# Compact inversion of the weight sums in the last attention, and layer norms that carry additions, clearing, loads and binarizing

## The reference

```python
x = x + jnp.tanh(g_xattn[3]) * _L3_xattn_ref(_layernorm(x, axis=-1), ctx_768, ...)
x = x + jnp.tanh(g_ffn[3]) * _L3_ffn_ref(_layernorm(x, axis=-1), ...)
```

```python
attn = jnp.einsum('bhqd,bhkd->bhqk', q, k) * scale
attn = jnp.clip(attn, -CLAMP, CLAMP)
attn = jax.nn.softmax(attn, axis=-1)
attn = jnp.where(jnp.any(jnp.isnan(attn)), jnp.asarray(1.0 / Nkv, attn.dtype), attn)
x = jnp.einsum('bhqk,bhkd->bqhd', attn, v).reshape(B, Nq, Cq)
return x @ Wo + bo
```

```python
alpha = mean(abs(w), axis=1, keepdims=True); bw = alpha * sign(w)      # _binarize
h = jax.nn.gelu(jnp.einsum('bsd,hd->bsh', x, bw1) + b1, approximate=False)
out = jnp.einsum('bsh,dh->bsd', h, bw2) + b2
```

## Time and profile before

| | |
|---|---|
| median of 3 runs | 4717.48 us (4715.63 to 4719.13) |
| the profiled execution | 4710.85 us, of it span 4709.2 us |
| last attention's loop, first clip to last | 3637 to 4591 us of the span |
| last norm and network | 4639 to 4705 us |
| mean granted TensorE clock | 0.892 of 2.4 GHz |

### The profile page before, as it was taken

One profiled execution on the slowest core, in us unless ns is written; L12 is line 12 of the kernel. 1 busy time (PEld: TensorE's weight loads), 2 busy tenths in 40 slices (PEclk: granted clock), 3 DMA queues, 4 the chain that ended last, 5 costly groups with the idle time before them and its releaser, 6 DMA issues. The chain is left out here.

```text
span 4709.2 us, 86688 instructions
## 1 busy us (share of the span) xinstructions
PE 3802.0 (81%) x32862; PEld 2475.0 (53%) x32862; DVE 2832.7 (60%) x3540; ACT 2051.6 (44%) x2875; POOL 1444.2 (31%) x1905
## 2 busy tenths in 40 slices
PE   7389889952557999997999996499585888888875
PEld 7156556631334666664666663277332555555553
DVE  8566555643335555534555543477546999989982
ACT  7166666630112434332343442266222666656651
POOL 0265344303213223212332310022005555545510
PEclk9689999976867999997999997799796999989996
DMA  6166666633413323312332320111004665556620
GB/s 165 44 149 151 136 140 146 149 104 134 149 24 90 87 79 85 80 47 62 87 87 79 86 61 15 41 44 31 17 0 100 138 137 129 133 124 138 138 71 14
DMA packets 197062, 434.60 MB, mean 92 GB/s; under 512 B 45708, under 2 KB 98878, under 8 KB 196589
## 3 DMA queue, kind: packets, MB, share of 16 engines
q1 hardware_dynamic: 122196, 338.87, 28.7%
q0 software_dynamic: 38912, 47.06, 4.7%
q10 hardware_dynamic: 35616, 43.97, 3.5%
HBM read 244.72 MB, written 32.67 MB: 59 GB/s over the span
## 5 line engine op out<-in xcount | busy, mean ns | idle before, releaser
L1401 DVE TENSOR_REDUCE L_mp<-ps 112x2 f32<-112x1000 f32 x384 | 458.2, 1198 | 549.4 <-PE ps L1223 545.9
L1260 PE MATMUL ps<-L_p,L_cn 125*97 125x448 f32 x1536 | 639.2, 538 | 0.0
L1384 ACT ACTIVATE L_p<-ps 125x896 f32<-125x896 f32 x384 | 352.2, 917 | 634.5 <-PE ps L1248 562.1
L2064 DVE TENSOR_REDUCE L_mp<-ps 112x2 f32<-112x1000 f32 x384 | 456.4, 1193 | 72.1 <-PE ps L1865 57.0
L2030 ACT ACTIVATE L_p<-L_p 125x896 f32<-125x896 f32 x384 | 364.8, 950 | 258.1 <-DVE L_p L2081 257.1
L885 ACT ACTIVATE L_p<-ps,rk 125x896 f32<-125x896 f32 x384 | 385.8, 1005 | 164.3 <-PE ps L763 144.9
L2081 DVE SCALAR_TENSOR_TENSOR L_p<-ps,xn 125x896 f32<-125x896 f32 x384 | 414.9, 1081 | 28.9 <-DMA xn<-L_low 20.2
L1246 PE MATMUL ps<-L_qh,L_ch 97*125 97x448 f32 x768 | 385.7, 502 | 14.2 <-DMA L_qh<-L_mc 14.2
L1260 PEld LDWEIGHTS ps<-L_p,L_cn 125*97 125x97 f32 x1536 | 250.4, 163 | 205.8 <-issue 165.9
L1897 PE MATMUL ps<-L_p,L_vs 125*18 125x112 f32 x6144 | 233.5, 272 | 120.2 <-ACT L_p L2030 104.5
L1223 PE MATMUL ps<-L_cr,L_qb 96*112 96x500 f32 x768 | 271.6, 440 | 37.8 <-DMA L_cr<-in_ctxT 32.6
(11 more groups left out here) (518 smaller groups left out, 7185.8 us busy)
## 6 DMA issues: line engine op xcount, KB each, us to landing
L_ks<-L_k_part SPq DMA_DIRECT2D x288, 375.0 KB, 9.7
L_ks<-L_k_first SPq DMA_DIRECT2D x96, 375.0 KB, 7.1
moe_w<-in_L_w SPq DMA_DIRECT2D x64, 512.0 KB
L_cn<-in_ctxN SPq DMA_DIRECT2D x32, 568.4 KB
cs_ct<-in_ctxT SPq DMA_DIRECT2D x32, 562.5 KB
L_raw<-in_ctxT SPq DMA_DIRECT2D x32, 562.5 KB
L_cr<-in_ctxT POOLq DMA_DIRECT2D x32, 562.5 KB, 4.8
L_ch<-in_ctxT POOLq DMA_DIRECT2D x32, 562.5 KB
```

The source lines that it names most:

```text
L1260: mm = nc.tensor.matmul(U[:, a, :], CN[s][:, j, :], P[:, n % 2, a * HALF:(a + 1) * HALF], start=(j == 0), stop=(j == KT - 1))
L1384: nc.scalar.activation(two(P[:, n % 2, :]), SB[n % 2], ACT.Exp).then_inc(S["exped"].sem, 1)
L1401: nc.vector.tensor_reduce(mp[:, 2 * k:2 * k + 2], ps[0:TT, bank:bank + 2, 0:500], AX.X, ALU.max).then_inc(S["chunk_maxed"].sem, 1)
L2064: nc.vector.tensor_reduce(mp[:, 2 * c:2 * c + 2], ps[0:TT, CB[pair], 0:500], AX.X, ALU.max).then_inc(S["chunk_maxed"], 1)
```

## The change

- `new_signals(True)` opens no block: the old semaphores are kept in `core.done`, and the next layer norm has GpSimd clear them beside its work.
- `add_gated` is gone. In the layer norms ahead of the four networks, VectorE adds one group of 448 columns at a time (`add`), and TensorE waits for each group before it makes its mean. The order on VectorE is add 0, add 1, centring 0, add 2, centring 1, add 3, centring 2, centring 3.
- `fold_weights` (second attention) and `quantize_weights` (third) give their loads to the layer norm ahead of them; in the former SyncE also waits there for their landing.
- `binarized_mlp` runs its layer norm itself and gives it the loads, the sign (ahead of the squares on ScalarE), the binarizing (between centring and inversion on VectorE), the transposes (behind the spreads on TensorE, now in banks 5 and 6) and the copy (at the end on VectorE).
- In the last attention the sums are picked out by four small matmuls with `UE` as weights into 112 partitions x 16 columns. VectorE inverts those 16 columns once, behind the clip of step 3. ScalarE widens them to 2 x 256 columns (`widen`, ahead of the key part and the exp of step 5; they are stored in `RD` and `UN`), TensorE transposes and spreads them with four matmuls at step 5 (`spread`), and ScalarE copies the 448 columns to `RD` ahead of the exp of step 7 (`take_sums`).

```diff
-        if old:
+        if later:
+            self.done += old
+        elif old:
...
+            if done:
+                @block.gpsimd
+                def _(pool):
+                    nc.clear_and_free_semaphores([s.sem for s in done])
...
                 for c in range(NCH):
+                    if gated:
+                        pe.wait_ge(added.sem, added.at(c + 1))
                     nc.tensor.matmul(ps[:, c, 0:CH], core.J[:, :], src[:, columns(c)],
...
+                if aside:
+                    aside.tensor(pe)
...
+                if aside:
+                    aside.scalar(act)
                 for c in range(NCH):
                     act.wait_ge(cen.sem, cen.at(c + 1))
...
+                if gated:
+                    add(0)
                 for c in range(NCH):
+                    if gated and c + 1 < NCH:
+                        add(c + 1)
                     dve.wait_ge(mean.sem, mean.at(c + 1))
...
+                if aside:
+                    aside.vector(dve, link)
                 dve.wait_ge(cen.sem, cen.at(NCH))
                 dve.wait_ge(std.sem, std.at(1))
...
-    MISC = {0: ("keys", 0), 1: ("keys", 1), 2: ("keys", 2), 3: ("pair", 0), 6: ("turn", 0),
+    MISC = {0: ("keys", 0), 1: ("keys", 1), 2: ("keys", 2), 3: ("pair", 0), 5: ("spread", 0), 6: ("turn", 0),
...
+            def pick_sums(b):
+                pe.wait_ge(S["u_copied"], b.lin(1, 2))
+                for c in range(4):
+                    mm = nc.tensor.matmul(ps[0:2 * NQ, 5, 4 * c:4 * c + 4], UE[:, c // 2, c % 2 * 2 * NQ:][:, 0:2 * NQ],
+                                          core.ident[:, DH:128:32], start=True, stop=True)
+                mm.then_inc(S["sums_picked"], 1)
 
             def spread_sums(b):
-                pe.wait_ge(S["u_copied"], b.lin(1, 2))
-                for j in range(2):
-                    mm = nc.tensor.matmul(of_head(ps[:, 5, 0:2 * QV], j), core.sum_row[:, j, :],
-                                          of_head(UE[:, :, :].rearrange("p s n -> p (s n)"), j),
-                                          start=True, stop=True)
+                pe.wait_ge(S["sums_widened"], twice_half_of(b, 2))
+                for c in range(4):
+                    mm = nc.tensor.matmul(ps[:, 5, c * 2 * NQ:(c + 1) * 2 * NQ],
+                                          wide(c // 2)[:, c % 2 * 128:(c % 2 + 1) * 128],
+                                          core.ident[0:2 * NQ, 0:2 * NQ], start=True, stop=True)
                 mm.then_inc(S["sums_spread"], 1)
...
+            def widen(b):
+                act.wait_ge(S["sums_inverted"], half_of(b, 1))
+                if b.turn is not None or b.r:
+                    act.wait_ge(S["u_normed"], b.lin(1, 0))
+                    act.wait_ge(S["projected"], half_of(b, 0))
+                for n in range(2):
+                    nc.scalar.activation(wide(n).rearrange("p (c g d) -> p c g d", c=2, g=4),
+                                         RC[:, 2 * n:2 * n + 2, :].unsqueeze(3).to_broadcast([2 * NQ, 2, 4, 32]),
+                                         ACT.Copy).then_inc(S["sums_widened"], 1)
...
+                    if n == 5 and b.r % 2 == 0 and (b - 2).there():
+                        widen(b - 2)
                     for at, c in ((5, 0), (7, 1), (8, 2)):
                         if n == at and (b + 3).there():
                             second_of_keys(b + 3, c)
...
-                nc.vector.reciprocal(RD[:, s, :], ps[:, 5, s * QV:(s + 1) * QV]).then_inc(S["sums_inverted"], 1)
+                nc.vector.reciprocal(RC[:, :, :].rearrange("p c g -> p (c g)"), ps[0:2 * NQ, 5, 0:16]
+                                     ).then_inc(S["sums_inverted"], 1)
...
-        layer_norm(core, core.OT, core.xn, "o0", gamma_beta)
-        add_gated(core, core.xn, 0)
-        core.new_signals()
-        layer_norm(core, core.xT, core.xn, "f0")
+        layer_norm(core, core.OT, core.xn, "o0", gamma_beta)
+        core.new_signals(True)
+        layer_norm(core, core.xT, core.xn, "f0", gated=(core.xn, 0))
```

More of the change, by code:

```diff
@@ L70, in __init__ @@
         self.eps = self.sb("eps", [128, 1])
-        self.signals, self.part = [], 0
+        self.signals, self.done, self.part = [], [], 0
         self.new_signals()
@@ L217, in _, with add @@
                 link = core.linker(dve, "dve")
+                def add(c):
+                    tile, gate = gated
+                    nc.vector.scalar_tensor_tensor(out=core.xT[:, columns(c)], in0=tile[:, columns(c)],
+                                                   scalar=core.tg[:, gate:gate + 1], in1=core.xT[:, columns(c)],
+                                                   op0=ALU.mult, op1=ALU.add).then_inc(added.sem, 1)
+                if gated:
+                    add(0)
                 for c in range(NCH):
+                    if gated and c + 1 < NCH:
+                        add(c + 1)
                     dve.wait_ge(mean.sem, mean.at(c + 1))
@@ L229, in _ @@
                     finish(link)
-        for s, n in ((mean, NCH), (cen, NCH), (sq, NCH), (var, 1), (std, 1), (inv, 1), (spread, NCH)):
+                if aside:
+                    aside.vector_last(dve, link)
+        for s, n in ((added, NCH if gated else 0), (mean, NCH), (cen, NCH), (sq, NCH), (var, 1), (std, 1), (inv, 1), (spread, NCH)):
             s.base += n
[L234 to L243, removed]
 CS = 4
@@ L416, in fold_weights, with load @@
         nw = 16 * len(loads)
-        with nc.Block() as block:
[L418 to L422, removed]
+        def load(sp):
+            for dst, name in loads:
+                sp.dma_start(dst, d[f"{L}_{name}"]).then_inc(w_in.sem, 16)
+            sp.wait_ge(w_in.sem, nw)
+        if norm:
+            norm(load)
+        with nc.Block() as block:
+            if not norm:
+                block.sync(load)
             if N is None and not keep_max:
@@ L1610, in misc @@
         kind, n = MISC[k]
+        if kind == "spread" and b.r % 2:
+            return None
         if kind == "pair":
             kind = "project" if b.r % 2 else "sums"
-        of = {"values": b + 1, "keys": b + 3, "turn": b + 1, "sums": b - 2, "project": b - 3}[kind]
+        of = {"values": b + 1, "keys": b + 3, "turn": b + 1, "sums": b - 2, "spread": b - 2, "project": b - 3}[kind]
         if not of.there():
@@ L1849, in fifth_bank @@
                 if kind == "sums":
+                    pick_sums(of)
+                if kind == "spread":
                     spread_sums(of)
@@ L1954, in _ @@
             pe.wait_ge(*emptied("project", 0, last - 2))
+            pick_sums(last)
             spread_sums(last)
@@ L2014, in empty @@
                     copy_turned(of)
+                if kind == "spread":
+                    take_sums(of)
                 if kind == "project":
@@ L2049, in _ @@
             copy_sums(Eight(None, B - 1))
+            widen(Eight(None, B - 2))
+            take_sums(Eight(None, B - 2))
             out(Eight(None, B - 2))
@@ L2104, in body @@
                         clip_tile(b + 1, k + 2 - KT)
-                    if b.r % 2 == 0 and (b - 2).there() and k in (3, 4):
-                        invert(b - 2, k - 3)
+                    if b.r % 2 == 0 and (b - 2).there() and k == 3:
+                        invert(b - 2)
             first = Eight(None, 0)
@@ L2122, in _ @@
             batches(dve, body)
-            for s in range(2):
-                invert(Eight(None, B - 2), s)
+            invert(Eight(None, B - 2))
             dve.wait_ge(S["u_normed"], B)
@@ L2607, in loads @@
             sp.dma_start(wd[:, :, :], d[f"{L}_wd"]).then_inc(S["wd_in"], 16)
-        layer_norm(core, core.xT, core.xn, tag, loads=loads)
+        layer_norm(core, core.xT, core.xn, tag, loads=loads, gated=gated)
         with nc.Block() as block:
@@ L2878, in quantize_weights, with load @@
         w_in, summed, spread = (core.sig(f"bitw_{n}") for n in ("in", "summed", "spread"))
+        def load(sp):
+            for n in BW:
+                sp.dma_start(w[n][:, :, :], d[f"bit_{n}"]).then_inc(w_in.sem, 16)
+        if norm:
+            norm(load)
         with nc.Block() as block:
-            @block.sync
-            def _(sp):
-                for n in BW:
-                    sp.dma_start(w[n][:, :, :], d[f"bit_{n}"]).then_inc(w_in.sem, 16)
+            if not norm:
+                block.sync(load)
             @block.tensor
```

110 lines of the change are left out of this document (61 added, 49 removed).

## The result

The changed kernel takes 4658.8 us (median of four, 4651.6 to 4677.9) against 4716.6 of the kernel before (four runs): a ratio of 0.9885, 95% interval 0.9855 to 0.9916, so 54 us less, between 40 and 68. A second comparison of the same two gave 4664.9 against 4711.1, ratio 0.9905 (0.9887 to 0.9922), 45 us less, between 37 and 53. Forecast were 4670 and 48 us.

What follows compares the result with a forecast made beforehand. No engine was full over the span; VectorE bound odd batches, even ones were slowed by TensorE's clock, and nothing overlapped at seams. Seams 34 plus loop 14 made 48 us off the 4717.48 median: 4670, range 4645 to 4698.

Steps and rivals of the forecast that it cites:

- seam term: Where blocks end and layer norms begin: additions, clearing, loads and last stage together save 34 us, bounds 27 to 43.
- loop term: Last attention's loop: 1.1 us saved per pair of batches, 15 in all, minus 1.5 at the tail: 14 us.
- Additions: Four seams with an addition ahead of a norm: quarter additions overlapping the norm save 2.0 us each, 8 in all.
- Clearing: Four other seams: semaphore clearing beside the norm saves 0 to 0.94 us each, taken as 2 in all.
- Loads: Weight loads covered by the preceding norm: 11.1 us saved at the second attention, 5.7 at the third.
- Last stage: Final norm to first matmul: 13.45 us now, new sum 6.4 including a 2.95 later inversion, so 7.1 saved.
- The failed term: Even batches of the last attention: TensorE falling to 1.2 GHz costs 1.3 us, counted for half, so 0.6 per pair.
- Limits and keys: Last attention's loop: transfers of limit vector and keys lose the slow stretch as slack, costing 0.3 us per pair.
- Tail: End of the last attention, at 1.2 GHz: a longer chain of pick, invert, widen, spread and copy loses 1.5 us.
- The second (the loop gives nothing, the clock falls each time): Rival for the last attention's loop: exponential 5 late, clock falling each time, only seams count; 4683.5 us, chance 0.22.
- The first (clock holds everywhere): Rival for the last attention's loop: the clock holds, the loop gives 26.5 us, time 4657; chance 0.24.
- The third: Rival: the new gap keeps TensorE at 1.2 GHz from tile 5 to 10; slower, 4766 us, chance 0.05.

Runs made afterwards that it cites:

- the second execution: The changed kernel profiled again, unaltered, with the second comparison against the kernel before: span 4654.4 us, median 4664.9 us, ratio 0.9905.
- the first execution: The changed kernel's first profiled execution, the longest of its four: 4677.9 us, span 4676.3 us.
- the seams alone: The whole change, but with the last attention's loop as in the kernel before: 4671.9 us, ratio 0.9918 to the kernel before.
- gap-filled kernel: The changed kernel plus five matmuls of 500 columns, results unread, in TensorE's idle piece of even batches: 4639.2 us, ratio 0.9853.
- the kernel with the earlier turn: The changed kernel with ScalarE's widening moved behind tile 5's exponential and the limits' turn at place 4 instead of 6: 4601.2 us, ratio 0.9767.
- the loop alone: The last attention as changed, all seams as in the kernel before: 4707.7 us, ratio 0.9991 to the kernel before.
- the long gap: The changed kernel with widening behind tile 5's exponential, plus fourteen small ScalarE copies ahead of that exponential in even batches: 4690.9 us, ratio 0.9948.
- the widening later: The changed kernel with ScalarE's widening one place later, behind tile 5's exponential: 4616.9 us, ratio 0.9798 to the kernel before.
- the old gap: The changed kernel with widening behind tile 5's exponential, plus seven small ScalarE copies that make that exponential late again: 4667.4 us, ratio 0.9915.

## Why the prediction came out, point by point

The total was right in part by luck: a seam term that was too small and a loop term that was too large nearly cancelled. In both, the term mis-sized most is TensorE's clock.

**Additions.** Forecast 8 us, 2.0 each. The four blocks take 5.87, 7.09, 5.88 and 6.98 us in the profile (9.43, 9.98, 9.82 and 9.26 before): 12.7 saved. I had put the last centring's end at 7.1 to 8.0. The step that failed is the first mean, "its centring 1.87 us later": that row was taken at a granted clock of 0.50, and I used it for all four blocks. In the second and the fourth block the clock is 0.50 there again; the first centring starts 2.64 us behind the first addition (forecast 2.6), and quarter 3's addition ends at 5.35 and 5.25 (forecast about 5.4). In the first and the third the clock is 1.00: the first mean takes 1.05 us, the first centring starts at 1.79, and quarter 3's addition ends at 4.14 (1011.90 + 0.68 - 1008.44). Ahead of these four means TensorE idled 6.05, 4.11, 4.46 and 8.95 us before, with 0.50 in all, and 3.26, 1.44, 1.81 and 6.21 us now. As the 1.44 us go with 0.50 and the 3.26 with 1.00, the idle time alone doesn't decide it; what does isn't shown.

**Clearing.** Forecast 2 for four seams. Two of them went from 0.93 to 0.33 (between the gated experts' last addition and the next norm's mean), the first experts' from 1.45 to 0.54, the first attention's from 5.56 to 4.77: 2.9.

**Loads.** The second attention's term was exact: 11.65 to 0.52. The third's was 5.64 (forecast 5.7). What I counted at 0, TensorE coming warm into the 13 us of folding, is real but not steady. The 64 matmuls took 13.1 us at a granted clock of 0.50 before, 11.5 at 0.60 in the profile, and in the second execution 6.9 at 1.00: 2 to 6 us more. Of the ten profiles with the new seams six have 6.9 us there, and four 11.3 to 11.5.

**Last stage.** 13.45 - 2.34 = 11.1 less behind the norm, 5.40 - 2.66 = 2.7 more ahead of the inversion (forecast 2.95): 8.4 saved, not 7.1. The transposes took 1.04 us, not the 1.97 of the row of before (TensorE now comes from the spread at 2.4 GHz), and end 0.14 us after the last product, where I had them stick out by 1.3. One term I hadn't at all: the network behind that first matmul takes 36.6 us in the first execution and 35.4 in the second, against 38.0 before, at a mean granted clock of 0.92 and 0.97 against 0.90; that is 1.4 to 2.6 more.

Together 12.7 + 2.9 + 11.1 + 5.6 + 8.4 = 40.7, with 2 to 6 for the fold and 1 to 3 for the network 44 to 50. The run with the seams alone says 39 (32 to 46), the forecast said 34. So the parts as read give more than the run. Ahead of the last attention the first execution saves only 21.5 us (first clip at 3615.98 instead of 3637.45) where its parts give 31.7, the second 33.5 of 36. What takes the rest back lies in the stages between the seams, which differ from profile to profile: from the fold's first matmul to the second addition pass 1499.5 us before, 1502.3 in the first execution and 1493.6 in the second.

**Loop.** Forecast 14, measured 4 (-2 to 10) alone, 7 to 13 as the difference of medians, 7.6 by the spans of the second execution and -0.7 by those of the first. What the steps say:

- The late exponential is the step that I had: forecast 1.45 us, measured 1.34. The idle piece "from 0.42 to 2.46" is 1.88 us long.
- If the clock holds: forecast 12.9, measured 12.42. VectorE waits 1.26 and 0.17 us for maximum 5 and 6 there (forecast 1.4 and 0.3): weigh 5 starts 2.33 us behind the clip's end instead of 2.46, and from its chunk to weigh 6 pass 1.86 us instead of 1.96. The two rows, of the batch in which the clock held:

```profile
4054.73 1.20 DVE L2131 TENSOR_REDUCE L_mp<-ps 112x2 f32<-112x1000 f32 x1 [1.26 <-PE ps L1908]
...
4057.10 1.20 DVE L2131 TENSOR_REDUCE L_mp<-ps 112x2 f32<-112x1000 f32 x1 [0.17 <-PE ps L1908]
```

- The failed term is the clock's. I counted 1.3 us in half of the batches. The clock falls in 13 of 14, and each fallen stretch is (198.09 - 12.42) / 13 - 12.42 = 1.9 us longer (2.2 in the first execution). That is 1.7 per pair instead of 0.6, 16 us more over 14 pairs, against 7 for the better stretch. The gap-filled kernel prices it directly.
- Limits and keys: forecast 0.3 per pair, 4 us. The waits for these two transfers were 20.2 + 6.7 us before, and are 23.6 + 12.0 in the first execution, 21.7 + 9.1 in the second: 4 to 9 us more, so up to 5 beyond the forecast. I had set 5 as the mark of error; one execution is above it. That the limits hold up the loop is shown by the kernel with the earlier turn: with the limits sooner, VectorE's wait for them fell by 13 us and the loop by 31 in its profile (16 by the medians).
- Tail: forecast 1.5 us lost. From the last clip to the end of the last projection pass 10.6 us before, 11.2 and 11.6 in the two executions: 0.7 to 1.0 lost.

Together 14 - 16 + 7 - (0 to 5) and under 1 back from the tail: 0 to 6, beside the 4 of the loop alone.

**Signs.** The idle piece of 1.9 us ended by the exponential and the covered loads came as said. The even stretches of 14.45 and 14.15 us lie nearer to the 14.9 that I had named as a sign of error than to 13.5, which is the clock's term again. "6 to 7 us from the last norm to its first matmul" was wrong as written: of the sum of 6.4, 2.95 lie ahead of the inversion, so its own terms give 3.4; 2.34 were measured, with the transposes at 2.4 GHz.

**Rivals.** The second (the loop gives nothing, the clock falls each time) described the mechanism better than the forecast: 13 falls of 14, the loop's worth 4 to 13. The first (clock holds everywhere) was not the kernel's state, but filling the gap produces it; that kernel takes 4639, not 4657, as the seams gave more and a stretch is 12.42 us, not 12.9. The third was tried with the long gap and didn't come. As to the rule of the Trainium skill that I set beside the second ("TensorE: Matmul & The Clock Gate", section "A second HAM failure mode: psum-queue depth-cycling"): the trace agrees that short idle times make TensorE's clock go up and down, and adds that here it is a matter of degree; that each gap is a fall was my reading of the page, which calls the idling frequent enough and names no length. In the kernels with such a piece, one of 1.9 to 2.1 us went with a fall in 11 of 13 to 13 of 14 batches, one of 1.1 to 1.6 in 3 of 14, one of 0.6 to 0.7 in none of 13; yet up to four pieces of 0.6 to 1.0 us close behind each other, as before, went with a fall in all 14.

**Left open.** Why the clock held in batch 14 in both executions of the changed kernel, and why in just that batch it fell once with the widening later, no run here tells. Nor do they tell what makes the three falls that come before the idle piece, nor the one fall in an odd stretch in the first execution (12.70 us instead of 11.1, granted clock 0.92) and in the kernel with the old gap (12.48 us, 0.93). I did not try the seams' parts one by one; their shares are read from the profile and checked only by their sum.

## What to carry to other kernels

Shortening an operation gains nothing if what it feeds is queued ahead of the critical work on another engine: the changed kernel saved 45 us of VectorE and put 1.3 us ahead of an exponential; one place later the same widening held nothing up, and the kernel was 48 us faster. Read the clock beside every duration that a forecast takes from a TensorE row: 1.87 us at 1.2 GHz was 1.05 at 2.4. When work is moved to a helper engine, write down for each step what is queued behind it there, and choose the place where the next critical operation is still waiting for something else. Where TensorE's clock falls in a loop, fill or remove its one idle piece first: five matmuls with results thrown away made this kernel 26 us faster.

## What the runs showed of the hardware

How often TensorE's granted clock fell went with the length of the one idle piece by degrees and not by a sharp bound: of 14 stretches each, none fell with a piece of 0.82 to 0.95 us (the filled gap), 3 with 1.11 to 1.29, 3 with 1.37 to 1.56, 11 to 13 with 1.9 to 2.1, 14 with 2.6. Extra, useless work on TensorE shortened the loop (PE busy 11.17 us per stretch against 11.91, at 2.4 GHz). And the state in which TensorE enters a stage is worth microseconds there: the same 64 matmuls of the fold took 13.1 us at 1.2 GHz behind 12.39 us of idleness. Behind 1.25 us they took 6.9 us at 2.4 GHz in six profiles, but 11.3 to 11.5 in four; what made that difference isn't shown.
